# State space of a fused convolution, whitening and scan kernel: Silus and softplus over more steps, remainders of B and C by PE, last projection in halves, constants loaded in the whitening

## The reference, cut to what matters

```python
xz = xn @ W_in.T                       # xn: layer norm of the whitened image
xi, z = split(xz, 2)
xc = silu(conv_b + sum(shift(xi, k) * conv_w[:, k] for k in range(4)))   # causal, u
dt, Bm, Cm = split(xc @ W_x.T, [4, 4 + 16])
delta = softplus(dt @ W_dt.T + b_dt)
A = -exp(A_log)                        # 128 x 16
h = h * exp(d_t * A) + (d_t * u_t) * B_t     # for each pixel t, 16 states n
y_t = sum_n(h * C_t)
out = ((y + xc * Dp) * silu(z)) @ W_out.T + x
```

## Time and profile before

| | us |
|---|---|
| median of 3 runs | 3678.57 (3675.59 to 3679.82) |
| profiled execution, its own time | 3668.06 |
| its span | 3666.4 |
| mean granted clock of PE | 0.948 |
| PE busy | 3163.0 (86%) |
| DVE busy | 2573.4 (70%) |
| POOL busy | 2214.4 (60%) |
| ACT busy | 2006.1 (55%) |

### The profile page before, as it was taken

The page is one execution under the profiler, slowest core; times in us unless marked ns, Lnnn a source line. Parts: engine busy times, 40 slices in busy tenths (PEclk is TensorE's granted clock), DMA queues, the critical chain, the costliest instruction groups (busy, mean ns, idle before and its releaser), DMA issues. The chain is left out here.

```text
span 3666.4 us, 55668 instructions
## 1 busy us (share of the span) xinstructions
PE 3163.0 (86%) x18550; PEld 1183.9 (32%) x18550; DVE 2573.4 (70%) x3346; ACT 2006.1 (55%) x2381; POOL 2214.4 (60%) x684
## 2 busy tenths in 40 slices
PE   6999999999999999999995899774888888887787
PEld 2333333333333333333331233341322222222222
DVE  5777777777767777777771222142888988988988
ACT  3566666666656666666663333223555564565554
POOL 0577777777777777777776000003657666666666
PEclk7899999999999999999998999886989999999999
DMA  2000000000000000000003211114333433443443
GB/s 103 12 16 10 16 16 16 16 13 16 16 17 10 16 16 16 19 10 16 16 10 74 92 69 46 48 64 149 119 132 128 155 142 120 153 150 118 147 150 115
DMA packets 74739, 234.86 MB, mean 64 GB/s; under 512 B 13088, under 2 KB 14180, under 8 KB 74420
## 3 DMA queue, kind: packets, MB, share of 16 engines
q1 hardware_dynamic: 69460, 215.06, 17.3%
q0 software_dynamic: 5056, 16.83, 1.3%
HBM read 192.42 MB, written 39.39 MB: 63 GB/s over the span
## 5 line engine op out<-in xcount | busy, mean ns | idle before, releaser
L526 DVE TENSOR_REDUCE at_pmax<-at_ring 128x1 f32<-128x512 f32 x2048 | 1300.8, 685 | 392.0 <-PE at_ring L334 381.2
L479 ACT ACTIVATE at_probs<-at_sc 128x1024 f32<-128x1024 f32 x1024 | 992.5, 1021 | 531.7 <-PE at_sc L402 529.7
L580 POOL TENSOR_TENSOR at_prob_sums<-at_prob_sums,at_probs 128x2048 f32<-128x2048 f32 x256 | 1159.0, 4527 | 74.8 <-ACT at_probs L479 54.5
L398 PE MATMUL at_sc<-at_QT,at_KT 32*128 32x512 f32 x4096 | 782.5, 634 | 4.1 <-issue 3.7
L1634 POOL TENSOR_TENSOR ss_drive<-ss_du,ss_bsb 128x1024 f32<-128x1024 f32 x261 | 610.7, 2352 | 263.9 <-DVE ss_state L1591 257.1
L1534 ACT ACTIVATE ss_decay<-ss_delta,ss_a 128x512 f32<-128x512 f32 x520 | 354.5, 687 | 447.6 <-DVE ss_state L1587 299.5
L410 PE MATMUL at_O<-at_probs,at_V 128*32 128x512 f32 x4096 | 535.3, 606 | 52.5 <-DVE at_att L549 51.6
L580 POOL TENSOR_TENSOR at_prob_sums<-at_probs 128x2048 f32<-128x2048 f32 x64 | 290.7, 4543 | 403.1 <-ACT at_probs L479 403.1
L1423 PE MATMUL ss_Y<-ss_seen,ss_ident 128*128 128x512 f32 x1032 | 520.7, 628 | 0.0
L334 PE MATMUL at_ring<-at_KH,at_QH 32*128 32x512 bf16 x2048 | 442.3, 387 | 5.7 <-DVE at_pmax L526 2.9
L1599 DVE TENSOR_TENSOR ss_seen<-ss_state,ss_C 128x1024 f32<-128x1024 f32 x259 | 316.3, 1221 | 80.4 <-PE ss_C L1411 72.6
(11 more groups left out here) (199 smaller groups left out, 2695.6 us busy)
## 6 DMA issues: line engine op xcount, KB each, us to landing
ss_bsb<-scratch_rows SPq DMA_DIRECT2D x265, 512.0 KB, 6.9
scratch_attn<-at_att SPq DMA_DIRECT2D x64, 256.0 KB, 2.0
fc_att<-scratch_attn SPq DMA_DIRECT2D x32, 512.0 KB, 5.8
ss_xn<-scratch_xm SPq DMA_DIRECT2D x34, 256.0 KB, 5.6
at_xn<-scratch_xn SPq DMA_DIRECT2D x32, 256.0 KB, 3.8
ss_xw<-scratch_xw SPq DMA_DIRECT2D x17, 256.0 KB, 3.9
ln_x<-in_x SPq DMA_DIRECT2D x8, 512.0 KB, 4.2
scratch_xn<-ln_xn POOLq DMA_DIRECT2D x8, 512.0 KB, 3.0
```

Source lines behind the costliest of these rows:

```text
L398: nc.tensor.matmul(sc[:, h, :], KT[head(h), par, blk(kb)], QT[head(h), par, hs(half)], start=True, stop=False)
L479: nc.scalar.activation(probs[:, kb, two, :].rearrange("p h q -> p (h q)"), sc[:, two, :].rearrange("p h q -> p (h q)"), ACT.Exp, scale=SCA ...
L526: nc.vector.tensor_reduce(pmax[:, quad // 2, h, quad % 2:quad % 2 + 1], ring[:, unit[3], :], AX_X, ALU.max, negate=True).then_inc(max_done, 1)
L580: nc.gpsimd.tensor_tensor(prob_sums[:, half, :, :], before, probs[:, k, :, :], ALU.add).then_inc(pool_sums, 1)
```

## The change

- Silu of u and Silu of z stand in different steps (6 and 14), each with its own two table loads. The gate of image 0 is taken in step 1 of that image.
- `W_dt` and the dt rows of `W_x` are multiplied at the start of the phase into one 128 x 128 matrix, `ss_w_delta`. DT becomes a product of u with it; the copy `ss_dt` is gone.
- The bf16 parts of B and C: PE forms `W_x` times u again and takes away the high part by a matrix that is minus the identity (`less`, `take_away`), ACT rounds what is left to the middle part; once more for the low part. `ss_bc_rest` on DVE and `low` on POOL are gone.
- Softplus is in two parts, in steps 11 and 12.
- The last projection is in halves, in steps 1 and 2. ACT's copy stands at the end of step 2 and waits for both.
- On PE z waits for `relu_done`, B and C for `u_done`, DT for `low_done`. X is in step 5 and was in step 6. The order on `ss_aux` is now X, B and C, two take-aways, DT, z.
- The 12 constants are loaded by SP at the end of its program in the whitening (`load_next`); they have their own buffers from there on.
- The clearing of `ss_xn` covers its first 3 columns only, and `ss_bc` is cleared.

```diff
-        AT_X, AT_CONV, AT_Z, AT_BC, AT_REST, AT_MID, AT_DT, AT_LOW, AT_DELTA = 6, 6, 8, 9, 10, 11, 12, 12, 13
+        AT_X, AT_BC, AT_LESS_HI, AT_LESS_MID, AT_DT, AT_Z = 5, 7, 8, 9, 11, 13
+        AT_PRE, AT_U, AT_HI, AT_MID, AT_LOW, AT_ABS, AT_LN, AT_GATE = 5, 6, 7, 8, 9, 11, 12, 14
+        AT_ROWS, AT_DELTA = 10, 13
...
+            nc.tensor.matmul(Y[0:R, 0:DI], w_x[:, 2 * N:], ident[:], start=True, stop=True).then_inc(xr_ready, 1)
+            pe.wait_ge(xr_done, 1)
+            nc.tensor.matmul(Y[:, HALF:HALF + DI], w_xr[:], w_dt[0:R, :], start=True, stop=True).then_inc(delta_w_ready, 1)
...
+                        m = nc.tensor.matmul(aux[:, hs(h)], w_delta[:], u_in[:, par, hs(h)], start=True, stop=True)
...
+            def take_away(b, par, part):
+                if part == 0:
+                    pe.wait_ge(hi_done, b + 1)
+                    pe.wait_ge(brow_done, b + 1)
+                else:
+                    pe.wait_ge(mid_done, b + 1)
+                for h in range(2):
+                    nc.tensor.matmul(aux[0:2 * N, hs(h)], w_x[:, 0:2 * N], u_in[:, par, hs(h)], start=True, stop=False)
+                    for k in range(part + 1):
+                        m = nc.tensor.matmul(aux[0:2 * N, hs(h)], less[:, k, :], bc[:, par, hs(h)], start=False, stop=(k == part))
+                m.then_inc(mid_taken if part else hi_taken, 1)
...
+            def project_out(b, par, h):
+                if h == 0:
+                    pe.wait_ge(y_step, b + 2)
+                    pe.wait_ge(gate_done, b + 2)
+                    pe.wait_ge(xw_in, (b + 1) * DMA)
+                nc.tensor.matmul(aux[0:C, hs(h)], w_out[:], yv[:, hs(h)], start=True, stop=False)
+                m = nc.tensor.matmul(aux[0:C, hs(h)], ident[0:C, 0:C], xw[:, par, hs(h)], start=False, stop=True)
+                m.then_inc(out_ready, 1)
...
-                        if now[2] == 1:
...
+                        if now[2] in (1, 2):
+                            project_out(b, g, now[2] - 1)
...
+            def take_gate(b, par):
+                act.wait_ge(aux_ready, 4 * b + 4)
+                nc.scalar.activation(gate[:, par, :], aux[:], ACT.Silu).then_inc(gate_done, 1)
+                nc.scalar.preload_act_table_set("natural_log_exp_and_others")
+            def take_hi(b, par):
+                act.wait_ge(aux_ready, 4 * b + 2)
+                nc.scalar.activation(bc[0:2 * N, par, :], aux[0:2 * N, :], ACT.Copy).then_inc(hi_done, 1)
...
+                nc.scalar.activation(brow[:, par, :], aux[0:N, :], ACT.Copy).then_inc(brow_done, 1)
+            def take_mid(b, par):
+                act.wait_ge(hi_taken, b + 1)
+                nc.scalar.activation(bc[2 * N:4 * N, par, :], aux[0:2 * N, :], ACT.Copy).then_inc(mid_done, 1)
+            def take_low(b, par):
+                act.wait_ge(mid_taken, b + 1)
+                nc.scalar.activation(bc[4 * N:6 * N, par, :], aux[0:2 * N, :], ACT.Copy).then_inc(low_done, 1)
...
             def take_out(b):
-                act.wait_ge(out_ready, b + 1)
+                act.wait_ge(out_ready, 2 * b + 2)
...
-            nc.vector.memset(xn[:], 0.0).then_inc(cleared, 1)
+            nc.vector.memset(xn[:, 0:KC - 1], 0.0).then_inc(cleared, 1)
+            nc.vector.memset(bc[:], 0.0).then_inc(cleared, 1)
-            def take_rest(b, par):
-                dve.wait_ge(hi_done, b + 1)
-                nc.vector.tensor_tensor(bc_rest[:], aux[0:2 * N, :], bc[0:2 * N, par, :], ALU.subtract).then_inc(rest_done, 1)
...
+            load_next(sp)
```

More of the change, by code:

```diff
@@ L1242, in state_space_phase @@
         bc = sb("ss_bc", [P, 2, S], BF16)
-        bc_rest = sb("ss_bc_rest", [2 * N, S])
-        bc_mid = sb("ss_bc_mid", [2 * N, S], BF16)
-        dt = sb("ss_dt", [P, S])
+        less = sb("ss_less", [P, 2, 2 * N], BF16)
+        w_xr = sb("ss_w_xr", [R, DI])
+        w_delta = sb("ss_w_delta", [P, DI])
         soft = [sb(f"ss_soft{n}", [P, S]) for n in range(2)]
@@ L1335, in step @@
             def step(b, par, n):
-                if n == AT_REST:
+                if n == AT_ROWS:
                     write_rows(b + 1, 1 - par)
@@ L1390, in unit @@
                 elif k == 1:
-                    pe.wait_ge(pre_done, b + 1)
+                    pe.wait_ge(u_done, b + 1)
+                    for h in range(2):
+                        m = nc.tensor.matmul(aux[0:2 * N, hs(h)], w_x[:, 0:2 * N], u_in[:, par, hs(h)], start=True, stop=True)
+                elif k == 2:
+                    pe.wait_ge(low_done, b + 1)
+                    for h in range(2):
+                        m = nc.tensor.matmul(aux[:, hs(h)], w_delta[:], u_in[:, par, hs(h)], start=True, stop=True)
+                else:
+                    pe.wait_ge(relu_done, b + 1)
                     for h in range(2):
@@ L1430, in step @@
                 spread(Cp, N, b, par, n).then_inc(c_ready, 1)
-                for at, k in ((AT_X, 0), (AT_Z, 1), (AT_BC, 2), (AT_DT, 3)):
+                if n == AT_LESS_HI:
+                    take_away(b + 1, 1 - par, 0)
+                if n == AT_LESS_MID:
+                    take_away(b + 1, 1 - par, 1)
+                for at, k in ((AT_X, 0), (AT_BC, 1), (AT_DT, 2), (AT_Z, 3)):
                     if n == at:
                         unit(b + 1, 1 - par, k)
-            for k in range(4):
-                unit(0, 0, k)
+            def project_out(b, par, h):
[6 more added lines that the diff above has]
+                m.then_inc(out_ready, 1)
+            unit(0, 0, 0)
+            unit(0, 0, 1)
+            take_away(0, 0, 0)
+            take_away(0, 0, 1)
+            unit(0, 0, 2)
             for n in range(TURN):
@@ L1440, in _ @@
                     add_state(0, 0, n - 1)
+                else:
+                    unit(0, 0, 3)
             with pe.Fori(0, NB // 2) as j:
@@ L1463, in take_x, with take_u @@
                 nc.scalar.activation(pre[:], aux[:], ACT.Identity, bias=cols[:, 0:1]).then_inc(pre_done, 1)
-            def gates(b, par):
-                act.wait_ge(aux_ready, 4 * b + 2)
-                nc.scalar.activation(gate[:, par, :], aux[:], ACT.Silu).then_inc(gate_done, 1)
+            def take_u(b, par):
                 act.wait_ge(pre_done, b + 1)
@@ L1618, in _ @@
                         see(*now)
-                        if now[2] < TURN:
-                            finish(b, g, now[2])
-                        else:
-                            prepare(b + 1, 1 - g, now[2])
+                        finish(b, g, now[2])
         @block.gpsimd
@@ L1651, in step @@
                 make_drive(*ahead(b, par, n, LEAD))
-            low(0, 0)
             make_du(0, 0)
@@ L1663, in _ @@
                         step(*now)
-                        if now[2] == AT_LOW:
-                            pool.wait_ge(drive_done, b * N + AT_LOW + LEAD + 1 + DEPTH)
-                            low(b + 1, 1 - g)
                         if now[2] == AT_DELTA:
```

193 lines of the change are left out of this document (93 added, 100 removed).

## The result

The changed kernel takes 3704.82 us, median of 4 runs (3701.24 to 3707.63), against 3677.08 for the kernel before in the same session: ratio 1.0083, 95% interval 1.0070 to 1.0095, that is 0.8% slower. The forecast was 3698.6. The profiled execution took 3701.24 (span 3699.6, clock 0.949), which is 33.2 more than before's; the medians are 27.7 apart.

A forecast was written before the change was run, and what follows sets the result against it. DVE's work and its stalls were taken as the bound. Fifteen periods +22.5, first period -2.2, start -2 with 0.2 back, end +1.5 made +20.0: 3668.06 became 3688, plus 10.5 to the median 3698.6 us; 8-in-10 range 3660 to 3722.

The forecast's parts named there:

- The likeliest case: The ss_xn load is late and PE's clock falls: period 70.0 us for 68.5, time 3699 us; chance 0.52.
- ss_bc_rest, the halves: DVE saves 1.13 us an image; the split projection's stalls become 0.06 and 0.44, together 0.50 for 2.11.
- X waits on ss_xn: In step 5 X waits 3.3 us for its late load in 15 of 16 images; DVE stalls 3.3 to 3.4.
- The clock in the gap: PE idles before X and falls to 1.2 GHz; X and Y(4) lose 0.85 to 2.5 us, taken as 1.65.
- Rival B: The load is late but PE keeps 2.4 GHz: period 67.74 us, time 3664, faster; chance 0.13.
- Clock at diag: The clock falls at the diag product in some images, by the phase: +0.6 us a period.
- Take-aways: PE's remainder products in steps 8 and 9 make C late, stalling DVE 0.48 and 1.24 us; bounds 1.2 to 2.3.
- DT with 128 rows: The new DT product takes 1.8 us and the 2.01 us stall goes; taken as 0, bounds 0 to 2.0.
- Silus: Each ACT block with one Silu takes 3.65 us, 0.06 to 0.15 late at the gate; taken as 0.15.
- rival F: Every ACT table switch drains, about 1.38 us each: some 3780 us; chance 0.01.
- Z at step 13 fits: PE's z product in step 13 fits and adds no stall to the period.
- Start: Early constants gain 9.9 us, added take-aways and copies cost 8: net -2, bounds -5 to +2.

The follow-up runs named there:

- e1: The changed kernel with SP issuing the next image's ss_xn loads ahead of the ss_res store; 3622.2 us, ratio 0.9868 to the kernel before.
- e7: The kernel before with only the last projection in halves and X in step 5; 3747.84 us, ratio 1.0209 to the kernel before.
- e12: e7 with the ss_xn loads issued ahead of the ss_res store; 3631.8 us, ratio 0.9902 to the kernel before.
- e3: The changed kernel with four products that nobody reads (eight passes) on PE ahead of X's wait for ss_xn; 3672.23 us, ratio 1.0003 to the kernel before.
- e10: e9 with three products that nobody reads added on PE in step 15; 3607.53 us, ratio 0.9820 to the kernel before.
- e9: e1 with the two take-aways in steps 9 and 10 in place of 8 and 9; 3600.23 us, ratio 0.9793 to the kernel before.

## Why the prediction was right

The likeliest case came in: the load is late, PE's clock falls in the gap, and the kernel gets slower. The forecast was 6 us below the median measured. Its +20.0 stands against +27.7 between the medians and +33.2 between the profiled executions. Step by step:

- *ss_bc_rest, the halves.* As said: the part without stalls is 61.78 (61.98 forecast), and step 3 stalls 0.50, all of it there; the 0.06 of C(2) didn't show.
- *X waits on ss_xn.* The mechanism as said, in 15 of 15 images; shown by e1, e7 and e12. The size: 3.87 on the mean for 3.3. From the start of ss_res to the second landing 10.2 us pass in the image shown, for 9.4 forecast, and the issues come as soon after ss_res as in the earlier trace rows. It is the landing, some 6.4 after issue, where I had taken the 5.3 to 5.7 of one image; over the fifteen periods of the kernel before it was 5.0 to 6.8.
- *The clock in the gap.* The term mis-sized most: the step-6 stall was 6.37 on the mean for 5.04, of which the wait explains 0.57 and the clock the other 0.76. X took 5.1 to 6.7, so X alone lost up to 3.1 where I had allowed 2.5. Rival B, the same wait at 2.4 GHz, is what e3 comes near to at X: 3672 for its 3664, with a longer wait than B had, and with diag and z slow in some images, which B left out.
- *Clock at diag.* 1.82 in five images, 0.61 a period (0.6 forecast). The agreement is luck: the two falls in fifteen periods that the forecast names make 0.22 a period, and in other runs diag is slow in 0 (e10) to 12 (e9) images.
- *Take-aways.* 0.47 and 1.29 (0.48 and 1.24).
- *DT with 128 rows.* 1.88 us, and no stall from step 11 to 13.
- *Silus.* No stall at either (0.15 forecast). The load starts at 3210.07 and the Silu 1.30 behind it, about as in the earlier trace rows, and behind every table load of the state space of after it is 1.29 or 1.30. There is no drain, so rival F is out.
- *Not foreseen: z at step 13.* "Z at step 13 fits" holds at 2.4 GHz alone; in eight images the clock fell there and step 14 stalled 0.33 to 1.73, 0.43 a period. Step 12 leaves PE as bare as the steps before diag, and the prediction had priced a fall for diag only. The bare step alone isn't enough: in e9 it is as bare, with the take-aways one step nearer, and z never ran slow.
- *Start.* -7.1 for -2: X starts 6.3 into the stage (7 forecast), and X to the first scan is 38.0, 3.5 more than before and not 8. The forecast summed matmuls at half clock. In after the clock rises within the first take-away, and the first C row takes 0.60, where it took 1.03 in before; the mean clock from X to the first scan is 0.68 for 0.60. This isn't chance: it is 0.68 to 0.74 in the seven kernels with the take-aways and 0.60 to 0.65 in the seven without. The first period gave the -2.2 forecast.

The period's sum: 61.78 + 0.50 + 0.61 + 6.37 + 0.47 + 1.29 + 0.43 = 71.45, against 70.0. The 1.45 is 15 x 1.45 = 21.8 us too little in the periods, and the start (5.3 more gained than forecast), the earlier phases (2.5) and the end (0.7) took back 8.5 of it. So the period was under-forecast by 1.45 us, mostly at X, and the total came nearer than its parts by luck: errors of opposite sign. Of the 13.2 that are left by the profiled executions, 5.5 are gone between the medians, because before's profiled execution is 9.0 below its median and after's 3.6 below.

## What to carry to other kernels

When a change moves a consumer earlier, add up how much earlier it comes, how much later its producer's release gets, and compare with the slack of every transfer that it eats; parts that gain or cost nothing alone can lose together, as 0.9915 and 1.0013 made 1.0209. When one engine issues its DMAs in program order, put loads whose inputs are ready ahead of a store that waits for the last result; here it cost nothing where there was no wait and gave 2 to 3% where there was. Price a new gap on the matrix engine with the clock's fall behind it, and take the time that a load needs to land from all images, not from one.

## What the runs showed of the hardware

- The clock raised the price of a gap on PE by some two thirds: 3.87 us of waiting made 6.37 of stall. Useless products in the gap (e3) brought the stall to 4.1 and gave back 29 us of 3700.
- The clock fell in every second image of e10 and not in the others, with PE equally busy in the 4 us before (1.98 and 1.97 us).
- Products of a start-up chain ran at a higher clock with more work in it (mean granted clock 0.68 to 0.74 in seven kernels, for 0.60 to 0.65 in seven without the added work), though the chain got 3.5 us longer.
- The ss_xn landing spread over 4.9 to 7.4 us after issue in after (5.0 to 6.8 before); in the image shown the DMA share beside it was 0.94 to 1.03.
